# A block with a selective scan: channels outside and states inside a tile's partitions, last states copied by ScalarE, 12 of 32 driving products on GpSimd

## What is computed

```
x = x + sparse attention(norm(x))       16 heads of 8; window of 32 and every 64th row
x = x + three dense layers(norm(x))     weights of +1 and -1, 128 -> 512 -> 512 -> 128
x = x + scan block(norm(x))             below
x = x + three dense layers(norm(x))
```

```
dA = exp(dt_t[..., None] * A)
h = dA * h + (dt_t * u_t)[..., None] * B_t[:, None, :]
y_t = jnp.einsum('ben,bn->be', h, C_t)
```

## Time and profile before

| | us |
|---|---|
| median of 3 runs | 1010.6 |
| lowest and highest | 1006.17, 1012.24 |
| the profiled execution, its time | 1010.07 |
| its span | 1008.3 |
| TensorE busy | 777.3 |
| VectorE busy | 690.9 |
| ScalarE busy | 646.0 |
| GpSimd busy | 609.3 |

### The profile page before, as it was taken

How to read it: one execution, slowest core, us unless ns; L and a number is a source line. 1 busy time by engine, 2 the same in 40 slices (tenths; PEclk the granted TensorE clock), 3 DMA queues, 4 the chain that set the end, 5 groups by cost and what they waited for, 6 DMA issues and landing times. The chain is left out here.

```text
span 1008.3 us, 21855 instructions
## 1 busy us (share of the span) xinstructions
PE 777.3 (77%) x8036; PEld 433.7 (43%) x8036; DVE 690.9 (69%) x1138; ACT 646.0 (64%) x1282; POOL 609.3 (60%) x598
## 2 busy tenths in 40 slices
PE   7889889795959689795879868686948595848678
PEld 5665436343534265363543443343514341223336
DVE  7974468585948669682867777677768493747583
ACT  5786768694949669674668766576647353625343
POOL 4032457585739666682875576685759573947391
PEclk9999979897979979897889979697969798888779
DMA  4000122123121221222022222222222222222310
GB/s 163 4 3 2 58 110 109 74 95 118 61 102 43 108 93 74 88 77 102 34 105 87 102 110 93 106 84 101 93 85 77 107 73 102 77 102 88 117 69 22
DMA packets 41931, 83.60 MB, mean 83 GB/s; under 512 B 2009, under 2 KB 2658, under 8 KB 41826
## 3 DMA queue, kind: packets, MB, share of 16 engines
q1 hardware_dynamic: 41826, 82.22, 21.9%
HBM read 71.20 MB, written 11.01 MB: 82 GB/s over the span
## 5 line engine op out<-in xcount | busy, mean ns | idle before, releaser
L1803 POOL TENSOR_TENSOR d<-d,cr 128x1024 f32<-128x1024 f32 x128 | 299.7, 2350 | 46.4 <-issue 14.6
L1621 ACT ACTIVATE ps<-dt,An 128x512 f32<-128x512 f32 x252 | 172.2, 693 | 207.3 <-DMA dt<-dtd 137.5
L1292 DVE TENSOR_TENSOR d<-ps,du 128x512 f32<-128x512 f32 x173 | 114.2, 679 | 142.9 <-DMA du<-dud 72.6
L1304 DVE TENSOR_TENSOR_SCAN d<-ps,d 128x512 f32<-128x512 f32 x128 | 151.4, 1210 | 47.1 <-ACT ps L1621 42.9
L1304 DVE TENSOR_TENSOR_SCAN d<-ps,hl,d 128x512 f32<-128x512 f32 x128 | 158.3, 1267 | 26.1 <-ACT ps L1621 23.9
L1789 POOL TENSOR_TENSOR d<-du,br 128x512 f32<-128x512 f32 x79 | 99.7, 1271 | 106.0 <-DMA du<-dud 31.6
L885 PE MATMUL ps<-h,w 128*128 128x512 f16 (+1 forms) x512 | 123.8, 397 | 27.7 <-DVE h L1236 15.0
L885 PEld LDWEIGHTS ps<-h,w 128*128 128x128 f16 x512 | 49.5, 102 | 105.2 <-DVE h L1236 27.9
L974 PE MATMUL ps<-d,cst 128*32 128x512 f32 x512 | 75.5, 666 | 19.7 <-POOL d L1803 19.6
L823 PE MATMUL ps<-cst,sx 128*128 128x128 f32 x384 | 60.0, 297 | 27.2 <-ACT sx L1452 15.4
L896 PE MATMUL ps<-w,h 128*128 128x128 f32 x496 | 63.8, 285 | 12.7 <-ACT h L1518 12.7
(11 more groups left out here) (185 smaller groups left out, 1448.1 us busy)
## 6 DMA issues: line engine op xcount, KB each, us to landing
cr<-bcd SPq DMA_DIRECT2D x64, 256.0 KB
br<-bcd SPq DMA_DIRECT2D x64, 256.0 KB
dt<-dtd SPq DMA_DIRECT2D x64, 256.0 KB
du<-dud SPq DMA_DIRECT2D x64, 256.0 KB
dtd<-sR SPq DMA_DIRECT2D x16, 256.0 KB, 5.5
dud<-sE SPq DMA_DIRECT2D x16, 256.0 KB
X<-in_x SPq DMA_DIRECT2D x8, 256.0 KB, 6.0
out<-X SPq DMA_DIRECT2D x3, 512.0 KB, 12.5
```

Of the source, the lines that this page charges most:

```text
L1292: eng.tensor_tensor(d, PB[:, :], DU[:, q, :], ALU.mult).then_inc(v_dr, 1)
L1304: eng.tensor_tensor_scan(d, banks[u % NG][:, :], d, hl[:, r:r + 1] if m % 2 else 0.0, ALU.mult, ALU.add).then_inc(v_sc, 1)
L1621: eng.activation(banks[u % NG][:, :], src[:, :], ACT.Exp, scale=An[:, g:g + 1]).then_inc(s_da, 1)
L1803: eng.tensor_tensor(d, d, CR[k % NC][:, :].unsqueeze(1).to_broadcast((128, n, 512)), ALU.mult).then_inc(p_cm, n)
```

## The change

Six things are changed; of the table of places every number is drawn anew.

1. In a unit partition p now has channel p // 4 of the 32 and state p % 4. The source patterns of the four spread transfers have 32 as their first count and 4 as their second; before it was 4 and then 32. Bytes, number of transfers and tiles are the same.
2. The summing weights of csum_t, the `spread` matrix and the host's layout of A follow; `csel`, 32 columns, is added to the first load of weights.
3. The copy of last states is a step of its own, hl_s, on ScalarE. out_p waits for it, and so does the scan of the batch's second half.
4. GpSimd does the driving products of 12 of 32 units (14 and 30 are added), VectorE of 20; with unit 0 left out, 95 and 157 instead of 79 and 173.
5. WARM has 172 products in place of 220.
6. PLACES is new, so every engine's list is in another order.

```diff
-for _name, _n in (("ident", 128), ("qmask", 4), ("one8", 1), ("rmask", 2), ("spread", 128)):
+for _name, _n in (("ident", 128), ("qmask", 4), ("csel", 32), ("one8", 1), ("rmask", 2), ("spread", 128)):
...
-    put("spread", (p[:, None] % 32 == p[None, :] % 32).astype(np.float32))
+    put("csel", (p[:, None] // 4 == np.arange(32)[None, :]).astype(np.float32))
+    put("spread", (p[:, None] % 32 == p[None, :] // 4).astype(np.float32))
...
-DRIVEN_P = [0, 4, 6, 8, 12, 16, 20, 22, 24, 28]
+DRIVEN_P = [0, 4, 6, 8, 12, 14, 16, 20, 22, 24, 28, 30]
...
+    ([(u,) for u, in PAIRS if u // NR % 2 == 0], 'hl_s'),
...
             def states(k, at):
...
-                return bcd[k // 8 % 2][at:at + 4, :].unsqueeze(1).to_broadcast((4, 32, 512))
+                return bcd[k // 8 % 2][at:at + 4, :].unsqueeze(0).to_broadcast((32, 4, 512))
...
             def rows(src, n, q):
...
-                return src[n // 2 % 2][e:e + 32, :].unsqueeze(0).to_broadcast((4, 32, 512))
+                return src[n // 2 % 2][e:e + 32, :].unsqueeze(1).to_broadcast((32, 4, 512))
...
-                    t = eng.matmul(bank[32 * q:32 * q + 32, :], spread[:, 0:32], D[:, (4 * k + q) % ND, :],
+                    t = eng.matmul(bank[32 * q:32 * q + 32, :], csel, D[:, (4 * k + q) % ND, :],
...
                 if m % 2:
-                    eng.wait_ge(p_hl, NR * (m // 2) + r + 1)
+                    eng.wait_ge(s_hl, NR * (m // 2) + r + 1)
...
+            def hl_s(u):
+
+                r = u % NR
+                eng.wait_ge(v_sc, u + 2)
+                eng.copy(hl[:, r:r + 2], D[:, u % ND:u % ND + 2, 511]).then_inc(s_hl, 2)
...
                 if m % 2 == 0:
-                    eng.tensor_scalar(hl[:, r:r + 2], d[:, :, 511], 1.0, 0.0, ALU.mult, ALU.add).then_inc(p_hl, 2)
-                    eng.wait_ge(p_hl, NR * (m // 2) + r + 2)
+                    eng.wait_ge(s_hl, NR * (m // 2) + r + 2)
                 eng.tensor_tensor(d, d, CR[k % NC][:, :].unsqueeze(1).to_broadcast((128, n, 512)), ALU.mult).then_inc(p_cm, n)
...
-    al = a["attn_b_A_log"].reshape(2, 4, 32, 4, 4).transpose(4, 2, 0, 3, 1).reshape(128, 32)
+    al = a["attn_b_A_log"].reshape(2, 4, 32, 4, 4).transpose(2, 4, 0, 3, 1).reshape(128, 32)
```

More of the change, by code:

```diff
@@ L428 @@
-    "store_d": [448837, 707994, 724379, 739111, 749903, 755287],
+    "aap_p": [14076, 67339, 224936, 402030],
+    "aback_v": [51741, 86247, 178809, 218413, 327988, 364979, 497826, 555192],
+    "afar_v": [22650, 25455, 29215, 29558, 32547, 49272, 50937, 51280, 111431, 118846, 119189, 144546, 149291, 159498, 174746, 175089,
+        259516, 271575, 271918, 283766, 299627, 299970, 321311, 323381, 433670, 449535, 449878, 465878, 466221, 486886, 487229, 495310],
+    "akd_v": [12399, 14530],
+    "akp_p": [13866, 136352, 223425, 451459],
@@ new lines @@
+    "aln_p": [5113, 7233, 24274, 37863, 68589, 139499, 285159, 310351],
+    "aln_s": [9909, 10881, 63763, 64240, 213568, 222698, 389660, 394708],
+    "aln_t": [8849, 10192, 60289, 60780, 210800, 222009, 387218, 394019],
+    "aln_v": [22993, 36582, 67044, 73454, 85108, 256457],
+    "an_s": [44818],
+    "ano_s": [7142, 9124, 54669, 56209, 160293, 202160, 350265, 384221],
+    "aown_s": [22220, 22872, 27796, 28273, 31864, 37695, 42917, 43089, 44596, 44707, 51549, 53330, 53441, 53552, 53663, 54087, 68561,
[5 rows of a table added]
@@ new lines @@
+    "dt_p": [111075, 129173, 179021, 194901, 265091, 282499, 349522, 382307, 437214, 456819, 498221, 518923, 584234, 606744, 656244,
+        675409],
+    "dt_s": [109271, 126958, 176998, 191988, 263287, 279996, 347008, 380482, 435410, 454351, 495947, 516205, 582385, 602718, 653974,
+        670701],
+    "dt_t": [108117, 125804, 175452, 190834, 262133, 278602, 345610, 379039, 434256, 452705, 494793, 515051, 581231, 601564, 652804,
+        669317],
+    "dt_v": [110565, 128663, 178429, 193282, 264581, 281660, 348520, 381776, 436704, 456036, 497446, 517499, 583679, 605324, 655731,
[6 rows of a table added]
@@ new lines @@
+    "du_d": [115859, 137036, 185447, 202411, 270844, 301958, 354717, 393309, 442409, 468017, 505884, 538968, 590513, 611945, 662523,
+        685387],
+    "du_p": [114555, 132653, 184143, 201107, 269540, 300654, 353413, 386756, 441105, 463178, 504580, 526837, 589209, 610641, 661219,
[33 rows of a table added]
+    "fln_p": [64493, 116415, 216859, 267751, 303932, 328502, 384967, 405595, 488894, 533935, 581144, 604955, 634930, 649672, 698273,
+        738804, 741600],
+    "fln_s": [68084, 126431, 221095, 272376, 314902, 367962, 390350, 414200, 510747, 538883, 589122, 610767, 656426, 684187, 713673,
+        742043, 746768],
@@ new lines @@
+    "fln_t": [67422, 125340, 220433, 271409, 313039, 367300, 389688, 413183, 510085, 538221, 588460, 610105, 653855, 671457, 709338,
+        741600, 746325],
+    "fln_v": [63207, 115129, 215485, 266283, 302646, 316119, 377423, 399994, 485745, 532553, 577018, 602392, 632855, 645584, 691376,
+        737995, 740667],
+    "flo_v": [68703, 130882, 221714, 273678, 315521, 368740, 392830, 415144, 511494, 539654, 589924, 612132, 657118, 686538, 714425,
+        742448, 747173],
+    "fno_s": [66365, 122960, 218731, 269707, 306739, 364331, 387507, 407888, 499499, 535856, 585205, 607560, 638624, 664857, 703377,
+        740668, 744405],
@@ new lines @@
+    "jrec_v": [55998, 102983, 204028, 251829, 355832, 377123, 521331, 592057],
+    "jsub_p": [53094, 88257, 185380, 223635, 336646, 369159, 505927, 582933],
+    "jsum_p": [54843, 101025, 202344, 248656, 354650, 375968, 517844, 590446],
+    "jtr_v": [60535, 107520, 209835, 261181, 366793, 382753, 527685, 597133],
+    "jx_v": [62482, 114404, 214760, 265558, 372940, 392222, 531287, 601667],
+    "lg_v": [736352, 736694],
+    "lm_t": [736836, 737283],
+    "lm_v": [737480, 739504],
+    "lmo_t": [729478, 732999],
@@ new lines @@
+    "lpre_p": [716561],
+    "mln_p": [85250, 148681, 240719, 294101, 412014, 466730, 558523, 631923],
+    "mln_s": [89621, 157231, 246236, 299733, 417373, 474800, 562894, 636907],
+    "mln_t": [89775, 155457, 245419, 298975, 416662, 472109, 563048, 636448],
+    "mln_v": [83959, 147390, 239428, 292810, 410665, 461874, 557184, 630577],
+    "mno_s": [88025, 151509, 243669, 297055, 414789, 469840, 561298, 634698],
+    "mout_t": [217367, 293790, 387709, 464368, 557954, 610741, 683155],
+    "mout_v": [219630, 296217, 389792, 466564, 561907, 613924, 688923],
@@ new lines @@
+    "mu_s": [98869, 100069, 163159, 167494, 253000, 256093, 309386, 321884, 426024, 426607, 481420, 484214, 571279, 574714, 644053,
+        646764],
+    "mu_t": [91278, 96436, 158703, 163861, 249025, 252460, 305501, 318008, 418548, 421983, 476699, 480134, 567646, 571081, 639696, 643131],
+    "mx_d": [107263, 174819, 265065, 343264, 434223, 494760, 581198, 652771],
+    "mx_s": [106554, 174110, 261391, 330792, 433514, 494051, 580489, 652062],
+    "mx_t": [104437, 171322, 259193, 327817, 431144, 491240, 577814, 650131],
@@ new lines @@
+    "mxu_s": [137644, 183861, 287403, 300637, 422682, 545079, 615814, 718932],
+    "mz_s": [96313, 164975, 253583, 304034, 427190, 484897, 571862, 641390],
+    "mz_t": [94713, 162138, 247302, 302550, 425694, 483569, 565923, 637973],
+    "one_v": [13721],
+    "out_p": [122500, 126046, 137184, 143738, 146053, 152919, 159099, 162086, 164401, 166800, 173045, 175469, 186681, 188996, 191355,
[8 rows of a table added]
+    "out_v": [734162],
+    "scan_v": [119875, 121004, 123346, 124475, 127534, 129753, 135724, 137450, 138579, 139965, 142288, 143417, 144889, 152856, 153985,
[16 rows of a table added]
@@ L429 @@
+    "set_v": [39043, 77237],
+    "silu_s": [100851, 168077, 256676, 324611, 428627, 487652, 575297, 647347],
+    "store_d": [389635, 711384, 714536, 739615, 751798, 757182],
     "vz_p": [10085],
[L430 removed]
+    "yev_v": [170201, 203388, 242419, 287032, 331151, 374265, 426152, 458800, 493541, 540252, 573998, 606833, 648354, 679720, 716810],
 }
 WARM = [
[4 rows of a table removed]
[5 rows of a table added]
 ]
@@ L471, in const @@
             return cst[0:rows, at:at + n]
-        ident, qmask, one8, rmask, spread = (const(n) for n in ("ident", "qmask", "one8", "rmask", "spread"))
+        ident, qmask, csel, one8, rmask, spread = (const(n) for n in ("ident", "qmask", "csel", "one8", "rmask", "spread"))
         masks = sb("masks", [128, 288], BF16)
```

150 lines of the change are left out of this document (42 added, 108 removed), and 301 rows, old and new, of tables (PLACES, WARM).

## The result

| us | before | after |
|---|---|---|
| median | 1008.71 | 784.62 |
| lowest and highest | 1006.17, 1012.24 | 782.68, 786.93 |
| span of the profiled execution | 1008.3 | 781.6 |
| TensorE, VectorE busy | 777.3, 690.9 | 706.6, 679.2 |
| ScalarE, GpSimd busy | 646.0, 609.3 | 647.2, 614.5 |

The ratio is 0.7777, with a 95% interval of 0.7741 to 0.7814: 22% less time. The forecast was 845 us with a range of 812 to 905. The direction was right, the size was not: the kernel is faster than the lower end of the range.

The account below looks back on a forecast made before the run. Slow spread transfers, 2.45 us each, were taken to stall the units' stage. VectorE's 584.7 us at 85% busy gave 688 us; 132 + 688 + 23.3 made 843, with 1.8 around it 845 us; range 812 to 905.

Parts of the forecast that it names:

- What bounds the kernel: Units' stage: spread transfers at about 2.45 us each, slow by their DRAM pattern, stall every block; no engine is the bound.
- One engine for each step of the first count, up to 16: Spread transfers: first count 4 uses four engines, 26.2% share at 102 GB/s; first count 32 would use 16.
- The price of 0.72 us: One 262,144-byte spread transfer in the new layout, at the start loads' 363 GB/s, instead of 2.45 us.
- Eight transfers of dt and du against four units: At each block: eight transfers take 19.6 us against 13.3 or 10.8 us of four units; the rest is stall.
- The busy share of 85%: VectorE in the units' stage: 584.7 us busy at 85%, near the 83% of 34 low-traffic stretches, makes 688 us.
- The lower end of 812: Whole time if all 186.7 us of VectorE's named waits and 10.9 us of driving products go; below it, chance 0.02.
- Driving products and copies: VectorE loses 10.9 us, GpSimd gets 20.3 less 12.3, ScalarE 12.1; the copy's hand-over costs nothing unless decays wait for transfers.
- Half comes back: Rival: half the gain is given back to waits among the engines; about 911 us, 888 to 950; chance 0.13.
- Only dt and du: Rival: only dt and du get fast; br and cr stay at 2.45 us, waits of 73.1 us stay, 918 us; chance 0.03.
- Slower: Rival: layout changes nothing, GpSimd waits for ScalarE's copy behind decays that wait for dt; 1048 us; chance 0.02.
- The threshold of 1.35 us: Spread transfer's price, 10.8 us by eight, above which alone the rival of a slower kernel was to decide.
- The signs: Profile after: issues under 1 us, traffic well over 102 GB/s, dt wait under 30 us, VectorE 83 to 88%, TensorE 600 to 630 us.

Follow-up runs that it names:

- the layout alone: Parts 1 and 2 of the change put into the kernel before, its lists, engines and warming products kept: 780.64 us, ratio 0.7733; again 780.13 us.
- the dose: Kernel before, spread transfers cut after each buffer's first use to 256 or 384 of 512 columns, four engines kept: 808.6 us (0.8006) and 899.1 us (0.8900).

## Why the prediction was wrong, step by step

**What bounds the kernel: right.** Slow spread transfers, by their pattern. The layout alone gives all the gain, and the dose shows that the time follows the transfer's length.

**One engine for each step of the first count, up to 16: right, as far as 4 and 32 show it.** 94.0% against 26.2%. The page of the profile has a second, sharper sign: packets under 512 bytes went from 2009 before to 5081, by 3072, which is 256 transfers by 12. I read it as one small packet for each engine of a transfer, 4 before and 16 now. The earlier trace rows had it already: 16 such packets in 10 us, 4 for each of some 4 transfers. The Trainium skill says, in DMA: Bandwidth & Descriptors, section Why a DMA increments its semaphore by 16 and not by 1, that each engine of a transfer ends with a write of +1 to the semaphore. These counts agree with it, and with the section's rule for the number of engines.

**The price of 0.72 us: too low.** It is 0.90 in a row (290 GB/s). The loads of the earlier trace rows were not all of 256 KB as I wrote: one of 512 KB, issued at 3.99 us, took 6.1 us to land. Had the eight taken 7.2 instead of 5.8 us, with 4.0 us to landing instead of 3.0, the account of 8.8 us would have been 11.2, more than the 9.8 us of four units now (4 by 628/256). It fits all the same, since there is no wait for dt or du left. The code says why: each dt and du goes out when its own unit of the last four releases it, and its successor is needed four units after that unit. The account asked for all eight at once, which was too strict. The two misses cancelled, which was luck.

**Eight transfers of dt and du against four units: half right.** They carry most of it (183 of 229 us), but br and cr in the same queue are part of the stall, and by the estimate above nine to eleven transfers per block lie on the path.

**The busy share of 85%: the step that failed.** It made 584.7 us into 688. The busy time came to 581.3, and the share to 92.6%. At 85% the stage would have been 684 us and not 628: this one term holds 56 of the 60.4 us by which the forecast missed. I had taken the 83% from the 34 stretches that the transfers don't fill, as what the engines reach among themselves. I had said that they include the edges of the stalls, and allowed 2 points for them. The transfers' part in their idle time was larger. Two of them, waits of VectorE in the kernel before from 190 to 200 and from 420 to 430 us:

```profile
DVE d L1304 <- ACT ps L1621: 4.3, 2, 3.9
...
DVE d L1304 <- ACT ps L1621: 4.4, 2, 4.0
```

These are scans waiting for late decays, the very wait that I had put down to dt two paragraphs earlier. Summed over the 34 stretches, VectorE waited 20.2 us for decays, 8.1 without a releaser before the driving product, 3.0 for du, and 9.7 for the summing matmuls. Without the first three, 31.3 us, the share is 281.4 of 308.7, 91%; without the fourth too, 94%. The measured shares, 92.6% and 93.7%, lie between. I read it so: in a stretch with low traffic the late transfer has landed, and what it made late is still being waited for. Not every such wait is an echo, for 9.6 us of waits for decays stay in the layout alone. That the transfers, and not the lists, held the share down is shown by the layout alone: 93.7% with the old lists. How much of the rise came by way of TensorE's higher clock is open, as above.

**The lower end of 812: no bound,** though only 0.02 had been given to a time below it. It let only the named waits go, and kept the 70.7 us (257.4 less 186.7) as if they were the engines' own. 46.7 are left, and 39.6 in the layout alone. VectorE's wait for the summing matmuls, 16.5 us, fell to 3.6 and 5.5 though no matmul was moved in the layout alone. These matmuls had themselves been waiting; their rows (busy us, ns of one record, then the idle time before it) before

```profile
L974 PE MATMUL ps<-d,cst 128*32 128x512 f32 x512 | 75.5, 666 | 19.7 <-POOL d L1803 19.6
```

and in the layout alone:

```profile
L975 PE MATMUL ps<-d,cst 128*32 128x512 f32 x512 | 68.1, 604 | 2.7 <-POOL d L1804 2.7
```

The wait for GpSimd's product shrank from 19.6 to 2.7 us, and the mean record of one matmul from 666 to 604 ns, by 0.91. The granted clock went from 0.885 to 0.985 over the span, by 0.90. So TensorE's busy time, which I feared as the next bound, fell as the stalls went and the clock rose. I had read that from rows as 602 us; it came to 576.3, and 587.2 with the warming products.

**Driving products and copies: sizes right, effects wrong.** The rows are as costed: 0.676 us on VectorE, 1.275 on GpSimd, 0.196 for the copy on ScalarE. VectorE's busy time fell by 11.7 us, of which the layout alone brings 5.4 with no instruction moved, so that the forecast 10.9 matched partly by chance. But 10.9 us off the busiest engine brought 5 us in the new lists, and in the old ones, with GpSimd still copying, it cost 27. The hand-over, costed at nothing as long as decays don't wait for transfers, gains 11 us in the new lists and loses 22 in the old ones. Decays wait for no transfer in the first case and for 0.3 us in the second. Together with the new places these parts end 4.5 us behind the layout alone, where the sum gave them a gain of 10.9/0.85, 13 us.

**The rivals.** Half comes back: no. Only dt and du: no, for a transfer of B or C is as quick now as the others (3.3 and 3.2 us to landing, 4.0 and 3.6 for du and dt). Slower: with slow transfers the rest of the change costs 1.5%, but GpSimd's wait for the copy doesn't need them: with fast transfers and the old lists it is 55.7 us. The threshold of 1.35 us was too high: at 1.22 us there are still 28 us to lose.

**The signs.** Issues in a row under 1 us (0.52 to 0.60), traffic well over 102 GB/s (290), no wait for dt and copies at 0.196 us came as said. VectorE's 83 to 88% and TensorE's 600 to 630 us did not.

## What to carry to other kernels

Write a transfer that spreads few DRAM rows over many partitions so that its first count is large: 32 took all the engines here, 4 only four. A DMA share that stands at a quarter with a full queue is the sign to look for. When a stall is to go, don't take the busy share of the stretches around it for what is left: first subtract, wait by wait, what the same stall may have made late in them, and don't call the waits of later engines a floor. With the stall gone test each further part on its own, in the lists in which it is to stand: here the first part alone was the best kernel.

## What the runs showed of the hardware

- The number of small packets went with the number of engines of a transfer: 3072 more under 512 bytes for 256 transfers, 12 each, with 4 engines turned into 16.
- Sixteen engines are not four times four: 102 GB/s at 26.2% is 24 GB/s for one busy engine (102 / 4.19), 290 GB/s at 94.0% is 19 (290 / 15.0). A transfer went from 2.45 to 0.90 us, by 2.7.
- A summing matmul (128 x 512, float32) has a mean record of 666 ns before and 604 in the layout alone, with the span's granted clock at 0.885 and 0.985; removing stalls paid for part of TensorE's time as well.
- A copy of 128 x 2 took 0.196 us on ScalarE and 0.192 on GpSimd.
